# Eight adjacency units of a graph network's first pass go back into their own rows, and VectorE instead of TensorE sums them

## The chip, the cores and the metric

The kernel runs on one core of a Trainium2 chip. The metric is the device time of one execution in microseconds, the median of the runs.

## The reference

Four graph layers over one dense matrix adj of 8192 x 8192 float32 (256 MB) and node states x of 8192 x 64. Each layer normalises x, multiplies adj with the result and adds something made of the product to x, so layer l + 1 needs all of layer l for the columns that it reads:

```python
h = jnp.maximum(_layernorm(x, axis=-1), 0.0)
x = x + _L0_gnn_ref(h, adj, L0_gnn_u)               # adj @ (h * keep / 0.9)
h = jnp.maximum(_layernorm(x, axis=-1), 0.0)
x = x + _L1_gnn_ref(h, adj, L1_gnn_W, L1_gnn_b)     # (adj @ h + h) / deg, then W, relu, norm
h = jnp.maximum(_layernorm(x, axis=-1), 0.0)
x = x + _L2_gnn_ref(h, adj, L2_gnn_W)               # dinv * ((adj + I) @ (dinv * h)) @ W
h = jnp.maximum(_layernorm(x, axis=-1), 0.0)
x = x + _L3_gnn_ref(h, adj, L3_gnn_W)               # concat(h, adj @ h / (deg + 1)) @ W.T
```

The degrees deg are the row sums of adj, needed from layer 1 on.

## The kernel before, in words

adj is cut into 16 x 16 units of 512 x 512 (1 MB each). Unit (b, g) holds what row block b takes from source block g. The kernel makes several passes over the matrix; the change touches only the first (keys that begin with 1), some 760 of the 1857 us. In it the rows b = 0 to 15 are done in turn. For row b:

- the singles, sources g = 15 down to b + 1 (SINGLES): only layer 0 can take them, since the states of layer 1 for block g don't exist yet. `alone` (lines 783 to 791) makes 4 products of them, in one bank's lower half and another's upper half; the two halves of TensorE's columns work side by side.
- the late sources, g = 0 to b - 1 (LATE_SOURCES): here layer 1 is known too, and `both` (lines 793 to 800) makes 8 products of each, layer 0 in the lower half, layer 1 in the upper half of one bank, LOW[b]. A product is two instructions in the trace, so a single has 8 and a unit of both layers 16.
- the diagonal unit, which has two loads' slots of its own, with the layer 1 part of the row before.
- `finish(0, b - 1)` (line 830) after the first single of row b: it turns the sums of the row before for VectorE, which makes the next states of them (lines 1427 to 1432).

The degrees need the sum of every unit once. VectorE adds the units of DVE_SUMS into row_sum (line 1579, and line 1585 for the diagonal), and folds the row's sum at its end (lines 1590 and 1592), after which it begins the next row. After 5 sums of a row it ends layer 0 of the row before, with line 1431 and lines up to 1601. TensorE instead sums the units of PE_SUMS with `count_unit` (lines 840 to 844): 4 small products with a picking matrix into the bank DEG. In rows 4, 8 and 12, after the second single, `count_totals` (lines 846 to 852) adds VectorE's four folded rows to the same bank; it waits for the fold of the row before (total_ready).

The two orders that matter are written out by hand: `loads_in_order` (lines 236 to 253) is SP's order of loads, and TensorE's loop (lines 1195 to 1240) is its order of use. Loads go into a ring of 12 slots; SP loads slot n again when unit n - 12 has been released by TensorE (unit_freed) and, where VectorE sums it, by VectorE (unit_summed, lines 531 to 537).

Before the change two units each of rows 10 and 9 are taken out of their turn in each of rows 1 to 4 (EARLY): in row b, after the singles with index 8 and 9, come units (10, b - 1) and (9, b - 1). TensorE counts them and multiplies them for both layers into banks 4 and 6 (LOW[10], LOW[9]), which nothing else uses till rows 9 and 10 come. So rows 1 to 4 have 18 loads each, rows 9 and 10 have 12.

Of the kernel before, what the change touches and what calls it, by code (L numbers as in the profile page):

```python
# [9 lines left out]
ROWS = 16  # L10
# [20 lines left out]
SINGLES = [list(range(LAST, b, -1)) for b in range(ROWS)]  # L31

EARLY_ROWS = (10, 9)
EARLY = {b: [(r, b - 1) for r in EARLY_ROWS] for b in range(1, 5)}
AFTER_SINGLE = (8, 9)
EARLY_SOURCES = {b: [g for r, g in sum(EARLY.values(), []) if r == b] for b in range(ROWS)}
LATE_SOURCES = [[g for g in range(b) if g not in EARLY_SOURCES[b]] for b in range(ROWS)]
LOW = [b % 2 for b in range(ROWS)]  # L40
LOW[10], LOW[9] = 4, 6

PE_SUMS = [SINGLES[0][1:7]] + [EARLY_SOURCES[b] for b in range(1, ROWS)]
DVE_SUMS = [[g for g in SINGLES[b] + list(range(b)) if g not in PE_SUMS[b]] for b in range(ROWS)]


# [5 lines left out]
def upper(job):  # L52
    return LAST - 1 - job[0], LAST - job[1]


def lower(job):
    return job
# [35 lines left out]
def step_loads(p, kind, n):  # L93

    hi, lo = PAIRS[p]
    if kind == "cover":
        return [(2, 0, n)]
    if kind == "four":
        s1, s2 = FOURS[p][n]
        return [(2, lo, s1), (2, lo, s2), (2, hi, s1), (2, hi, s2)]  # L100
    if kind == "near":
        return [("again", *PAIRS[p - 1][::-1]) if p else (2, 0, CUT), (2, lo, hi)]
    return [(2, hi, n), (2, lo, n)]
# [132 lines left out]
def loads_in_order():  # L236
    out = []
    for b in range(ROWS):
        for i, g in enumerate(SINGLES[b]):
            out += [(1, b, g)]  # L240
            if b in EARLY and i in AFTER_SINGLE:
                out += [(1, *EARLY[b][AFTER_SINGLE.index(i)])]
        out += [(1, b, g) for g in LATE_SOURCES[b][:-1]] + [("diag", 1, b)]
        out += [(1, b, b - 1)] if b else []
    out += [(2, *upper(job)) for step in FIRST_A + FIRST_C for job in step]
    for p, (hi, lo) in enumerate(PAIRS):
        for kind, n in PAIR_STEPS[p]:
            out += step_loads(p, kind, n)
    out += [(2, 0, g) for g in COVER_AT_END[:-1]] + [("again", *PAIRS[-1][::-1]), ("again", 0, CUT),
                                                  (2, 0, COVER_AT_END[-1])]  # L250
    out += [(3, *lower(job)) for step in FIRST_A + FIRST_C for job in step]
    return out + down_loads()
# [35 lines left out]
def gnn_stack(nc, x_in, u_in, stream_in, w1_in, b1_in, w2_in, w3_in, x_out):  # L288
# [6 lines left out]
    with ctx:  # L295
# [111 lines left out]
        def half_of(bank, half):  # L407
            return banks[bank][half * F:(half + 1) * F, :]
# [50 lines left out]
        def source_tile(buf, k):  # L459
            return buf[:, k * COLS:(k + 1) * COLS]  # L460

        def slot(key):
            return ring[PLACE[key] % RING]

        def loaded(key):
            return unit_loaded[PLACE[key] % RING], 16 * (PLACE[key] // RING + 1)
# [4 lines left out]
        def diag_arrived(phase, b):  # L471
            n = DIAGS["diag", phase, b]
            return diag_loaded[n % 2], 16 * (n // 2 + 1)
# [7 lines left out]
        def state(layer, b):  # L481

            return h_ready, 1 + PROLOGUE.index(b // TPR) if layer == 0 else QUARTERS + rank(layer - 1, b) + 1
# [290 lines left out]
        def _(pe):  # L774
            def mm(bank, half, layer, J, moving, start, stop):
                return nc.tensor.matmul(half_of(bank, half), h[layer % 2][:, J], moving, start=start, stop=stop)  # L776

            def await_unit(key, *layers):
                pe.wait_ge(*loaded(key))
                for layer in layers:  # L780
                    pe.wait_ge(*state(layer, key[2]))

            def alone(key, layer, low, high, first, last_low, last_high, fresh_low=True):

                for k in (0, 2):
                    J = key[2] * TPR + k
                    mm(low, 0, layer, J, source_tile(slot(key), k), first and fresh_low and k == 0,
                       last_low and k == 2)
                    done = mm(high, 1, layer, J + 1, source_tile(slot(key), k + 1),
                              first and k == 0, last_high and k == 2)  # L790
                done.then_inc(unit_freed, 1)

            def both(key, layer, bank, first, first_next, last, last_next):

                for k in range(TPR):
                    J = key[2] * TPR + k
                    mm(bank, 0, layer, J, source_tile(slot(key), k), first and k == 0, last and k == TPR - 1)
                    done = mm(bank, 1, layer + 1, J, source_tile(slot(key), k),
                              first_next and k == 0, last_next and k == TPR - 1)
                done.then_inc(unit_freed, 1)  # L800
# [35 lines left out]
            def pick(b):  # L836

                return picker[:, F - 1 - b:F - 1 - b + QUARTER]

            def count_unit(key):  # L840

                for k in range(TPR):
                    nc.tensor.matmul(DEG[k * QUARTER:(k + 1) * QUARTER, :], pick(key[1]), source_tile(slot(key), k),
                                     start=key == (1, 0, PE_SUMS[0][0]), stop=False)

# [350 lines left out]
            for b in range(ROWS):  # L1196
                low, high = LOW[b], 2 + b % 2
                if b >= 2:
                    pe.wait_ge(*gathered(0, b - 2))
                for i, g in enumerate(SINGLES[b]):  # L1200
                    await_unit((1, b, g), 0)
                    if g in PE_SUMS[b]:
                        count_unit((1, b, g))
                    alone((1, b, g), 0, low, high, i == 0, False, b > 0 and g == b + 1, not EARLY_SOURCES[b])
                    if i == min(1, LAST - 1 - b) and b > 0 and b % QUARTERS == 0:
                        count_totals(b - 1)
                    if i == 0 and b > 0:
                        finish(0, b - 1)
                    if b in EARLY and i in AFTER_SINGLE:
                        key = (1, *EARLY[b][AFTER_SINGLE.index(i)])  # L1210
                        await_unit(key, 0, 1)
                        count_unit(key)
                        both(key, 0, LOW[key[1]], b == 1, b == 1, False, False)
                if b >= 2:
                    pe.wait_ge(part_copied, PARTS.index((1, b - 2)) + 1)
                for g in LATE_SOURCES[b][:-1]:
                    await_unit((1, b, g), 0, 1)
                    both((1, b, g), 0, low, b == LAST and g == 0, g == 0, False, False)
                    if b == LAST and g == 0:
                        finish(0, b - 1)  # L1220
                    if b == LAST and g == 10:
                        count_totals(LAST)
                    if b == LAST and g == 11:
                        turn_degrees()
                    if b == LAST and g in (12, 13):
                        turn_own(1, 26 - g)
                pe.wait_ge(*diag_arrived(1, b))
                if b == 0:
                    for k in (0, 2):
                        mm(low, 0, 0, k, source_tile(diag_slot(1, b), k), False, k == 2)  # L1230
                        done = mm(high, 1, 0, k + 1, source_tile(diag_slot(1, b), k + 1), False, k == 2)
                    done.then_inc(diag_used, 1)
                else:
                    pe.wait_ge(diag_plus_one, b)
                    pe.wait_ge(*state(1, b - 1))
                    for k in range(TPR):
                        used = mm(low, 0, 0, b * TPR + k, source_tile(diag_slot(1, b), k), False, False)
                        done = mm(LOW[b - 1], 1, 1, (b - 1) * TPR + k, source_tile(diag_slot(1, b - 1), k),
                                  b == 1 and k == 0, k == TPR - 1)
                    used.then_inc(diag_used, 1)  # L1240
                    done.then_inc(diag_freed, 1)
                    if b == LAST:
                        turn_own(1, 12)
                    await_unit((1, b, b - 1), 0, 1)
                    both((1, b, b - 1), 0, low, False, b == 1, True, False)
# [10 lines left out]
            for k in (0, 1):  # L1256
                J = LAST * TPR + k
# [640 lines left out]
```

## Time and profile before

| | before |
|---|---|
| median of 3 runs | 1855.67 us (1855.26 to 1856.03) |
| the profiled execution | 1858.4 us, its span 1856.6 us |
| TensorE matmul busy | 1806.5 us, 97% |
| VectorE busy | 1461.4 us, 79% |
| DMA, mean | 365 GB/s |
| granted TensorE clock | 0.998 of full speed |

A row of the profile gives a group of instructions by line, engine, operation and what it writes and reads. Busy time is that of at least one instruction running; matmuls overlap, so the starts are a better measure than the sum of durations. In a timeline the number in brackets is the engine's idle time before, with what ended it.

### The profile page before, as it was taken

The page shows a single profiled execution, that of the slowest core. Times are in us where ns is not written, and L with a number is a line of the kernel's source. Part 1 is how long each engine was busy: PE and PEld are TensorE (multiplying, and loading weights), DVE is VectorE, ACT ScalarE, POOL GpSimd, SP SyncE. Part 2 cuts the span into 40 slices and gives each one's busy share as a digit, 9 for nine tenths or more (in the row PEclk, how much of TensorE's full clock was granted, in tenths as well). Part 3 has the DMA queues.
Part 4 walks back from the last instruction along what each step waited for, and adds up shares of the span by engine and source line. Part 5 has one row for each costly group of instructions (what it writes and reads, how often), then busy time and mean ns, then how long its engine had stood idle before and what let it go on. Part 6 is the DMA issues. An engine that isn't in the chain of part 4 may idle for free.

```text
span 1856.6 us, 21067 instructions
## 1 busy us (share of the span) xinstructions
PE 1806.5 (97%) x8392; PEld 624.2 (34%) x8392; DVE 1461.4 (79%) x1529; ACT 102.1 (6%) x270; POOL 9.1 (0%) x23
## 2 busy tenths in 40 slices
PE   5899999999999999999999999999999999999998
PEld 1223333333333333333333333333333333333333
DVE  8989899999997765669888664678878787877754
ACT  0000000000000000100000000111000000000000
POOL 0000000000000000000000000000000000000000
PEclk9999999999999999999999999999999999999999
DMA  9999999999988878298797798499899999999995
GB/s 384 421 421 421 421 421 421 421 421 421 416 333 319 318 282 298 70 408 329 293 393 317 302 365 333 167 366 420 347 422 374 421 383 421 421 393 421 421 421 236
DMA packets 96047, 676.79 MB, mean 365 GB/s; under 512 B 11216, under 2 KB 13264, under 8 KB 14288
## 3 DMA queue, kind: packets, MB, share of 16 engines
q1 hardware_dynamic: 93024, 673.23, 89.1%
q10 hardware_dynamic: 2928, 2.23, 0.4%
q8 instruction: 68, 1.11, 0.2%
q14 instruction: 27, 0.22, 0.0%
HBM read 673.32 MB, written 2.10 MB: 364 GB/s over the span
## 4 chain that ended last, share of the span: by engine, by line
PE 88%; DMA 7%; DVE 4%; issue 0%; SPq 0%; ACT 0%; DVEq 0%
PE acc L776 43%; DMA ring<-stream_in 7%; PE acc L976 5%; PE acc L950 5%; PE DEG L932 4%; PE acc L806 3%; PE HT L776 2%; PE acc L963 2%; PE Z L832 2%; PE acc L1162 2%; PE DEG L1174 2%; PE acc L1079 2%; PE acc L1055 2%; PE acc L1069 2%; PE acc L1110 1%; PE acc L1117 1%
## 5 line engine op out<-in xcount | busy, mean ns | idle before, releaser
L776 PE MATMUL acc<-ring,states 128*64 128x512 f32 x3984 | 901.7, 595 | 33.7 <-DMA ring<-stream_in 29.1
L776 PEld LDWEIGHTS acc<-ring,states 128*64 128x64 f32 x3984 | 286.8, 137 | 583.3 <-issue 553.3
L1579 DVE TENSOR_TENSOR row_sum<-row_sum,ring 128x2048 f32<-128x2048 f32 x194 | 444.6, 2292 | 14.7 <-DMA ring<-stream_in 9.7
L1703 DVE TENSOR_TENSOR ring<-row_totals,ring 128x2048 f32<-128x2048 f32 x27 | 61.8, 2289 | 56.1 <-PE DEG L934 55.9
L932 PE MATMUL DEG<-ring,states 128*64 128x512 f32 x216 | 99.2, 602 | 3.6 <-DMA ring<-stream_in 3.6
L950 PE MATMUL acc<-row_totals,row_sum 128*64 128x512 f32 x216 | 97.3, 593 | 2.7 <-DVE row_sum L1695 2.7
L934 PE MATMUL DEG<-ring,states 128*64 128x512 f32 x216 | 99.3, 603 | 0.0
L978 PE MATMUL acc<-ring,states 128*64 128x512 f32 x216 | 97.7, 595 | 0.0
L976 PE MATMUL acc<-ring,row_sum 128*64 128x512 f32 x216 | 97.7, 595 | 0.0
L952 PE MATMUL acc<-ring,row_sum 128*64 128x512 f32 x216 | 97.3, 593 | 0.0
L776 PE MATMUL acc<-diag,states 128*64 128x512 f32 x336 | 91.1, 594 | 0.6 <-DMA diag<-stream_in 0.6
L1675 DVE TENSOR_TENSOR row_totals<-ring 128x2048 f32<-128x2048 f32 x27 | 61.8, 2290 | 4.4 <-DMA ring<-stream_in 2.8
L1679 DVE TENSOR_TENSOR ring<-ring 128x2048 f32<-128x2048 f32 x27 | 61.9, 2292 | 1.1
L1712 DVE TENSOR_TENSOR ring<-ring 128x2048 f32<-128x2048 f32 x27 | 61.9, 2292 | 0.9
L832 PEld LDWEIGHTS Z<-below,y 128*128 128x128 f32 x384 | 47.0, 191 | 40.2 <-issue 28.0
L1657 DVE TENSOR_TENSOR y<-acc,y 64x512 f32<-64x512 f32 x65 | 44.4, 682 | 17.6 <-PE acc L776 15.5
L832 PE MATMUL Z<-below,y 128*128 128x64 f32 x384 | 52.4, 279 | 3.8 <-DVE y L1658 3.8
L950 PEld LDWEIGHTS acc<-row_totals,row_sum 128*64 128x64 f32 x216 | 29.2, 137 | 65.0 <-issue 57.3
L806 PE MATMUL acc<-ring,states 128*128 128x512 f32 x112 | 50.9, 601 | 0.0
L963 PE MATMUL acc<-ring,row_sum 128*64 128x512 f32 x108 | 50.7, 592 | 0.0
L965 PE MATMUL acc<-ring,row_sum 128*64 128x512 f32 x108 | 50.7, 592 | 0.0
L932 PEld LDWEIGHTS DEG<-ring,states 128*64 128x64 f32 x216 | 29.2, 139 | 63.7 <-issue 63.4
(207 smaller groups left out, 2087.0 us busy)
## 6 DMA issues: line engine op xcount, KB each, us to landing
ring<-stream_in SPq DMA_DIRECT2D x610, 1024.0 KB, 12.5
diag<-stream_in SPq DMA_DIRECT2D x28, 1024.0 KB, 13.2
x<-x_in SPq DMA_DIRECT2D x4, 512.0 KB, 7.0
y<-u_in SPq DMA_DIRECT2D x4, 512.0 KB, 8.9
x_out<-x ACTq DMA_DIRECT2D x16, 128.0 KB, 6.7
below<-w_in ACTq DMA_DIRECT2D x6, 16.0 KB, 5.7
bias<-b_in ACTq DMA_DIRECT2D x1, 32.0 KB, 10.0
```

The source lines that it names most:

```text
L776: return nc.tensor.matmul(half_of(bank, half), h[layer % 2][:, J], moving, start=start, stop=stop)
L806: done = nc.tensor.matmul(acc[bank][:, :], states[:, J * 2 * F:(J + 1) * 2 * F], source_tile(slot(key), k), start=first and k == 0, stop=l ...
L832: mm_z = nc.tensor.matmul(Z[:, t * F:(t + 1) * F], gathered_sums, below[:, layer - 1, :], start=True, stop=True)
L932: nc.tensor.matmul(down("P2"), h[0][:, a12[2] * TPR + k], source_tile(slot(a12), k), start=i == 0 and k == 0, stop=False)
L934: one = nc.tensor.matmul(down("P1"), h[0][:, a11[2] * TPR + k], source_tile(slot(a11), k), start=i == 0 and k == 0, stop=last and k == TPR ...
L950: nc.tensor.matmul(down("P5"), down_state(1)[:, k], source_tile(row_totals, k), start=i == 0 and k == 0, stop=last and k == TPR - 1)
L952: seven = nc.tensor.matmul(down("P7"), down_state(3)[:, k], source_tile(slot(a21), k), start=i == 0 and k == 0, stop=last and k == TPR - 1)
L963: nc.tensor.matmul(down("P4"), down_state(4)[:, k], source_tile(slot(a22), k), start=i == 0 and k == 0, stop=False)
L976: nc.tensor.matmul(down("P6"), down_state(2)[:, k], source_tile(slot(a11), k), start=i == 0 and k == 0, stop=last and k == TPR - 1)
L978: three = nc.tensor.matmul(down("P3"), h[1][:, a12[2] * TPR + k], source_tile(slot(a12), k), start=i == 0 and k == 0, stop=last and k == T ...
L1579: nc.vector.tensor_tensor(row_sum[:, :], before, slot(key)[:, :], ALU.add).then_inc(unit_summed, 1 if count > 1 else 2)
L1679: nc.vector.tensor_tensor(slot(a21)[:, :], slot(a11)[:, :], slot(a21)[:, :], ALU.subtract).then_inc(down_formed, 1)
```

## The change

The eight units stay in their own rows. The tables EARLY, AFTER_SINGLE and EARLY_SOURCES go, LATE_SOURCES holds all sources, all rows use banks 0 and 1, and PE_SUMS is empty apart from six units of row 0, so that DVE_SUMS holds the eight units. The loads and TensorE's loop lose the units in rows 1 to 4. All rows from 1 have 16 loads.

```diff
-EARLY_ROWS = (10, 9)
-EARLY = {b: [(r, b - 1) for r in EARLY_ROWS] for b in range(1, 5)}
-AFTER_SINGLE = (8, 9)
-EARLY_SOURCES = {b: [g for r, g in sum(EARLY.values(), []) if r == b] for b in range(ROWS)}
-LATE_SOURCES = [[g for g in range(b) if g not in EARLY_SOURCES[b]] for b in range(ROWS)]
+LATE_SOURCES = [list(range(b)) for b in range(ROWS)]
 LOW = [b % 2 for b in range(ROWS)]
-LOW[10], LOW[9] = 4, 6
-
-PE_SUMS = [SINGLES[0][1:7]] + [EARLY_SOURCES[b] for b in range(1, ROWS)]
+
+PE_SUMS = [SINGLES[0][1:7]] + [[] for b in range(1, ROWS)]
 DVE_SUMS = [[g for g in SINGLES[b] + list(range(b)) if g not in PE_SUMS[b]] for b in range(ROWS)]
...
         for i, g in enumerate(SINGLES[b]):
             out += [(1, b, g)]
-            if b in EARLY and i in AFTER_SINGLE:
-                out += [(1, *EARLY[b][AFTER_SINGLE.index(i)])]
...
-                    alone((1, b, g), 0, low, high, i == 0, False, b > 0 and g == b + 1, not EARLY_SOURCES[b])
+                    alone((1, b, g), 0, low, high, i == 0, False, b > 0 and g == b + 1)
...
-                    if b in EARLY and i in AFTER_SINGLE:
-                        key = (1, *EARLY[b][AFTER_SINGLE.index(i)])
-                        await_unit(key, 0, 1)
-                        count_unit(key)
-                        both(key, 0, LOW[key[1]], b == 1, b == 1, False, False)
```

`alone` loses its parameter fresh_low, with which rows 9 and 10 went on in a bank that was begun earlier.

## Rows read from the trace of the kernel before

**Rows 1.** The page: engines' busy time and share; GB/s in 40 slices.

```profile
PE 1806.5 (97%) x8392; PEld 624.2 (34%) x8392; DVE 1461.4 (79%) x1529; ACT 102.1 (6%) x270; POOL 9.1 (0%) x23
...
GB/s 384 421 421 421 421 421 421 421 421 421 416 333 319 318 282 298 70 408 329 293 393 317 302 365 333 167 366 420 347 422 374 421 383 421 421 393 421 421 421 236
```

**Rows 2.** Stretches cut by hand: end of row 0, rows 1, 3 and 7.

```profile
core 0: us, PE busy (x) PEld busy (x) DVE busy (x) ACT busy (x) POOL busy (x), PEclk, DMA share, GB/s
...
50.00:62.00 12.00, 9.80 (x44) 2.65 (x40) 10.28 (x6) 1.16 (x2) 0.00 (x0) 1.00 1.02 423
...
62.00:108.00 46.00, 41.63 (x195) 12.06 (x192) 43.23 (x31) 1.95 (x4) 0.00 (x0) 1.00 1.01 420
155.00:202.00 47.00, 45.37 (x217) 14.35 (x216) 42.03 (x29) 1.95 (x4) 0.00 (x0) 1.00 1.01 421
...
328.00:370.00 42.00, 42.00 (x199) 14.16 (x197) 40.75 (x30) 1.95 (x4) 0.00 (x0) 1.00 1.01 421
```

**Rows 3.** TensorE's waits (total us, times, longest): whole span, then 174 to 760 us.

```profile
PE acc L776 <- DMA ring<-stream_in: 29.1, 19, 19.6
...
PE acc L776 <- issue: 0.3, 1, 0.3
```

**Rows 4.** TensorE's timeline in rows 0 and 3 (start, duration, work, idle before).

```profile
57.23 1.94 PE L776 MATMUL acc<-diag,states 128*64 128x512 f32 x8 [0.55 <-DMA diag<-stream_in]
...
171.89 1.07 PE L843 MATMUL DEG<-ring,picker 128*32 128x512 f32 x8 [0.54 <-DMA ring<-stream_in]
172.89 5.37 PE L776 MATMUL acc<-ring,states 128*64 128x512 f32 x24
```

**Rows 5.** The chain that ended last, pieces in row 6 and row 11.

```profile
287.91 13.88 PE acc L776 x64
301.79 0.33 issue
...
480.41 48.22 PE acc L776 x224
```

**Rows 6.** VectorE's timeline: first sums of rows 1, 6, 7, 8; sums and fold between.

```profile
63.97 2.29 DVE L1579 TENSOR_TENSOR row_sum<-ring 128x2048 f32<-128x2048 f32 x1
...
237.12 2.29 DVE L1579 TENSOR_TENSOR row_sum<-row_sum,ring 128x2048 f32<-128x2048 f32 x1 [0.20 <-DMA ring<-stream_in]
...
284.31 2.29 DVE L1579 TENSOR_TENSOR row_sum<-ring 128x2048 f32<-128x2048 f32 x1
...
300.60 18.57 DVE L1579 TENSOR_TENSOR row_sum<-row_sum,ring 128x2048 f32<-128x2048 f32 x8
...
325.90 2.29 DVE L1579 TENSOR_TENSOR row_sum<-ring 128x2048 f32<-128x2048 f32 x1
...
366.71 0.69 DVE L1592 TENSOR_TENSOR row_totals<-row_sum 128x512 f32<-128x512 f32 x1
367.49 2.29 DVE L1579 TENSOR_TENSOR row_sum<-ring 128x2048 f32<-128x2048 f32 x1
```

**Rows 7.** TensorE's timeline, line 830 (ends the row before): starts in rows 7 to 12.

```profile
328.02 0.66 PE L830 MATMUL Z<-ident,y 128*128 128x128 f32 x4
369.96 0.66 PE L830 MATMUL Z<-ident,y 128*128 128x128 f32 x4
414.76 0.66 PE L830 MATMUL Z<-ident,y 128*128 128x128 f32 x4
446.40 0.66 PE L830 MATMUL Z<-ident,y 128*128 128x128 f32 x4
479.75 0.66 PE L830 MATMUL Z<-ident,y 128*128 128x128 f32 x4
528.56 0.66 PE L830 MATMUL Z<-ident,y 128*128 128x128 f32 x4
```

**Rows 8.** TensorE's timeline at the count of totals in row 8.

```profile
372.41 1.07 PE L851 MATMUL DEG<-row_totals,picker 128*32 128x512 f32 x8
```

**Rows 9.** Groups by line and form, 0 to 650 us: the counts of units.

```profile
L843 PE MATMUL DEG<-ring,picker 128*32 128x512 f32 x112 | 15.3, 617 | 1.7 <-DMA ring<-stream_in 1.7
```

More of the change, by code:

```diff
@@ L781, in await_unit, with alone @@
                     pe.wait_ge(*state(layer, key[2]))
-            def alone(key, layer, low, high, first, last_low, last_high, fresh_low=True):
+            def alone(key, layer, low, high, first, last_low, last_high):
                 for k in (0, 2):
                     J = key[2] * TPR + k
-                    mm(low, 0, layer, J, source_tile(slot(key), k), first and fresh_low and k == 0,
+                    mm(low, 0, layer, J, source_tile(slot(key), k), first and k == 0,
                        last_low and k == 2)
```

## The prediction

> **What bounds the kernel now.** I read the page first, its shares and its slices. The reader is to see that TensorE is busy nearly throughout and that the transfers run at 421 GB/s for the first quarter of the span and never again for so long [rows 1]. Then the stretches cut at the row boundaries: TensorE has idle time in rows 1 and 3 of the first pass and none in row 7, where VectorE is busy 40.8 us of 42 and the transfers still run at 421 GB/s; the granted clock is 1.00 everywhere [rows 2]. The waits say the same: TensorE lost 29.1 us to landings at line 776 in 19 waits, of which 19.57 us is the start, and after 174 us of the first pass nothing but 0.3 us of issue [rows 3]. So there are three suppliers of almost equal pace. A unit of the matrix lands every 2.49 us: TensorE's starved units start at 57.23 and 171.89 us, which are loads 15 and 61 of the stream counted from 0, so (171.89 - 57.23) / 46 = 2.493 us [rows 4]. A single (lines 783 to 791) takes TensorE 1.72 us (8 of them 13.88 us less one drain), a unit for both layers 3.44 us (224 instructions in 48.22 us, 16 to a unit) [rows 5]. A whole row takes VectorE 41.59 us where it waits for nothing: its first sums of rows 6 to 8 start 41.59 us apart [rows 6]. Sixteen landings take 16 x 2.49 = 39.8 us, so VectorE is slower than the landings in a row with no extra units. TensorE needs 29.8 + 1.72 b us for row b with all its sources (15 - b singles, b + 1 of both layers with the diagonal, 0.6 us of line 830); the traced starts of line 830 agree (row 7: 41.94; row 11: 48.81) [rows 7]. It is therefore below the landings up to row 5 and above from row 6.
>
> **Part 1, the eight units leave rows 1 to 4.** Each row has 16 landings instead of 18. TensorE is given 2 x 3.44 us of products and 2 x 1.00 us of counts less in each (a count of a unit, line 843, is 8 instructions; the next work starts 1.00 us after it) [rows 4]. All that was work in a stretch where it waits for landings at the end of the singles, so the removed work is worth nothing there; the landings are. After the change the last single of row b is load 16 b + 14 - b, and TensorE starts it when it lands or when its own work is done. Row 4: load 74 lands at about 204.9 us. From there 1.72 + 0.33 us (the single, and the gap in front of the units of both layers [rows 5]), 5 x 3.44 us of both layers, then nine singles and line 830 of row 5 (16.1 us) put the last single of row 5 at 240.2; it (load 89) lands at 242.1, so TensorE is starved. From that, 1.72 + 0.33 + 6 x 3.44 + 8 x 1.72 + 0.6 gives 279.2 for the last single of row 6; it is load 104, which lands at 237.12 + 17 x 2.49 = 279.4 (237.12 is the start of VectorE's sum of load 87, which it waited for) [rows 6]. So starvation ends just there, at 279.4. Before, TensorE starts the same single at 301.79 - 1.94 = 299.9 [rows 5]. TensorE is 20.5 us earlier at this place. That is about the eight landings (19.9 us).
>
> **Part 2, the eight units arrive in rows 9 and 10.** Both rows lie where TensorE has no idle time [rows 3], so each unit costs its full 3.44 us: 8 x 3.444 = 27.6 us. The rows took 31.64 and 33.35 us with 12 units (line 830 to line 830) [rows 7]; they become 45.4 and 47.1. Without anything else the sum would be 27.6 - 20.5 = 7.1 us slower. The landings don't hold these rows up: TensorE is some 17 us behind them in row 9, 22 in row 10 and 30 in row 11, which a ring of 12 slots (29.9 us of landings) still covers.
>
> **Part 3, VectorE sums the eight units.** 8 x 2.33 = 18.6 us more work [rows 6]. In rows 9 and 10 it is beside TensorE's longer rows (41.59 against 45.4 and 47.1 us), hence no cost. But in rows 1 to 4 VectorE loses what it had before: 18 landings (44.8 us) to do 41.59 us of work, with waits for the ring behind most sums [rows 6]. With 16 landings it never waits again. Its first sum of row 1 starts at 63.97 as before (row 0 is unchanged); the fifth needs load 21 (72.2 us) at 73.3, the closest place; from then it falls 1.8 us a row further behind the landings. So its row b starts at 63.97 + 41.59 (b - 1), row 4 at 188.7 and row 8 at 355.1.
>
> **Part 4, who waits for that.** Line 846, count_totals, makes TensorE wait in rows 4, 8 and 12, after the second single, for the fold of the row before on VectorE, and everything of TensorE's queue stands behind it. Row 4: TensorE comes there at about 187.1, the fold is ready at 188.6; the 1.6 us vanish, as it is starved later in that row. Row 8: in the trace of before the way from the last single of row 6 (299.9) to the count of row 8 (372.41) is 72.5 us [rows 5, 8], so TensorE comes to it at 279.4 + 72.5 = 351.9. The fold is ready at 355.0, 0.1 before the next row's first sum, and TensorE goes on at 355.1. Before, VectorE's fold was ready at 367.4 and TensorE came at 372.4, so this wait hid itself with 5 us to spare [rows 6, 8]. It is a new stall of 3.2 us, and no starvation comes later to absorb it. Row 12: VectorE at 521.5, TensorE at about 541, no wait. TensorE at the count of row 8 is thus 372.4 - 355.1 = 17.3 us earlier than before, and 27.6 - 17.3 = 10.2 us later after row 10.
>
> **Part 5, banks and what follows.** Rows 9 and 10 accumulate in banks 1 and 0 of all other rows, and take their waits for copies by ScalarE; neighbouring rows show no idle time for them [rows 3], so I cost it at 0 (bounds 0 and 0.3 us, the one issue gap). The pass ends in TensorE's work with the ring full, before as after, so the shift goes through to the end: nothing later starts from anything but the first pass's results and TensorE's releases. ScalarE and SP get no more to do; SP's loads change order only.
>
> The page on DMA of the Trainium skill (DMA: Bandwidth & Descriptors, Specifications) gives a limit of about 358 GB/s of HBM per core. The first pass moves 421 GB/s for 500 us, so the trace disagrees and decides [rows 1]. By the page a unit would take 2.93 us, the eight landings would be worth 23.4 us and the sum would be +4.1 us with VectorE ahead of the landings.
>
> **The sum.** The profiled execution took 1858.4 us with a span of 1856.6, 2.7 us over the median. +10.2 us gives a span of 1866.8 and a median of 1855.67 + 10.2 = 1865.9 us, 0.55% slower.
>
> **Rivals.** (a) VectorE doesn't gate: its fold of row 7 is ready before 351.9, or comes to be waited for only where there is slack. Then +7.1 us, 1862.8. Against it: a period of 41.59 that the trace repeats to 0.01 us [rows 6]. (b) VectorE is later: in row 1 it has only 1.0 us of margin to the landings, and some landings come 0.4 to 0.6 us late; each microsecond lost there appears as one at row 8. With 0.45 us lost in each of seven rows it is +13.3 us, 1869.0. (c) Faster, the other side: landings aren't what paces rows 4 to 6, TensorE stays fed after row 3 as now, and only its saved counts remain. That is 64 of the 112 count instructions of line 843, in eight units of 1.00 us [rows 4, 9]. Then -8.0 us, 1847.7. It decides where a landing takes less than row 4's work over its 16 units, 37.7 / 16 = 2.36 us; the rows show 2.49. (d) No change to measure: the two effects offset, as the eight landings and the lost wait in row 3 are worth nearly what the late units cost; it wants some 6 us more of gain in rows 1 to 6 than I find, and VectorE not to gate. +1 us, 1856.7.
>
> **How the numbers follow.** The forecast has 66%, with its own range of +9 to +12 us. (a) has 12%, (b) 10%, (c) 6%, (d) 6%. A difference of under 0.2% (3.7 us) can't be told from none by a measurement of this kernel. So faster 0.06, same 0.06, slower 0.88. The range leaves out (c) and (d) and reaches from below (a), 1861.5, to just over (b), 1869.5.
>
> **What would show each step.** Part 1: TensorE is starved in rows 1 to 6, the last time near 280 us, at gaps of 0.5 us that leave its granted clock at 1.00, as the like gaps of row 0 do [rows 2, 4]. Part 2: line 830 to line 830 of rows 9 and 10 at 45.4 and 47.1 us. Part 3: VectorE's first sums 41.59 us apart from 63.97 on, with no wait for the ring in between. Part 4: line 851 in row 8 starts near 355 and waited about 3 us for VectorE, with row 8's line 830 at about 349. If the first sum of row 8 starts before 352, (a) holds; if the last starved single is well before 240 us, (c) or (d) does; a wait of TensorE in rows 9 to 15 would break part 2 and make it slower still.

## The result, and the profile after

The changed kernel takes 1865.71 us (median of 4 runs, 1863.67 to 1867.1) against 1855.85 for the one before, a ratio of 1.0049 with a 95% interval of 1.0036 to 1.0061. That is 9.9 us slower, where 10.2 was forecast. The profiled execution took 1867.1 us with a span of 1865.2, against 1858.4 and 1856.6.

The page of the changed kernel, the lines that answer to [rows 1]:

```profile
span 1865.2 us, 20963 instructions
...
PE 1803.0 (97%) x8328; PEld 626.2 (34%) x8328; DVE 1479.7 (79%) x1537; ACT 102.0 (5%) x270; POOL 9.1 (0%) x23
...
GB/s 384 422 421 421 421 421 420 421 420 392 349 341 314 302 310 306 65 392 318 337 360 313 312 355 352 150 403 413 350 420 374 421 384 421 421 392 421 421 421 233
```

TensorE has 64 instructions less (the counts) and is busy 3.5 us less, VectorE 18.3 us more (eight sums), and the span is longer all the same. The transfers leave 421 GB/s a slice earlier, since TensorE falls behind them in rows 9 and 10: between 420 and 470 us SP waits 36.4 us for TensorE's releases of slots and 5.8 us for VectorE's.

TensorE's waits in the changed kernel (total us, times, longest), to lay beside [rows 3]; 19.3 us of the first line are again the start:

```profile
PE acc L769 <- DMA ring<-stream_in: 37.7, 36, 19.3
...
PE DEG L844 <- DVE row_totals L1580: 3.4, 2, 2.2
PE acc L769 <- issue: 3.4, 5, 1.0
```

36 waits for landings instead of 19, and one of a new kind: line 844 (line 851 before) waits for VectorE's folds. TensorE's timeline of the changed kernel from the end of row 6's singles, with line 823 (830 before) where it ends a row and line 844 at row 8's count:

```profile
267.40 13.95 PE L769 MATMUL acc<-ring,states 128*64 128x512 f32 x64
282.34 17.39 PE L769 MATMUL acc<-ring,states 128*64 128x512 f32 x80 [0.99 <-issue]
...
350.18 0.66 PE L823 MATMUL Z<-ident,y 128*128 128x128 f32 x4
350.77 1.94 PE L769 MATMUL acc<-ring,states 128*64 128x512 f32 x8
354.88 1.58 PE L844 MATMUL DEG<-row_totals,picker 128*32 128x512 f32 x8 [2.17 <-DVE row_totals L1580]
356.39 33.96 PE L769 MATMUL acc<-ring,states 128*64 128x512 f32 x152
...
398.87 0.66 PE L823 MATMUL Z<-ident,y 128*128 128x128 f32 x4
444.24 0.66 PE L823 MATMUL Z<-ident,y 128*128 128x128 f32 x4
491.33 0.66 PE L823 MATMUL Z<-ident,y 128*128 128x128 f32 x4
...
758.03 0.66 PE L823 MATMUL Z<-ident,y 128*128 128x128 f32 x4
```

The last line is the end of the first pass; in the kernel before it stands at 746.46. VectorE's first sums of rows 1, 7 and 8 (beside [rows 6]):

```profile
63.78 2.29 DVE L1567 TENSOR_TENSOR row_sum<-ring 128x2048 f32<-128x2048 f32 x1
...
313.32 2.29 DVE L1567 TENSOR_TENSOR row_sum<-ring 128x2048 f32<-128x2048 f32 x1
354.91 2.29 DVE L1567 TENSOR_TENSOR row_sum<-ring 128x2048 f32<-128x2048 f32 x1
```

(354.91 - 63.78) / 7 = 41.59 us a row: from row 1 to row 8 VectorE waits for no landing. Its only waits there are eight for ScalarE of at most 0.3 us each, which it had before too. The count at 354.88 starts when its fold is ready.

The difference of the two traces adds up place by place. At row 8's count TensorE is 372.41 - 354.88 = 17.5 us earlier. From there to the end of row 8 it takes 398.87 - 354.88 = 43.99 us, where it took 414.76 - 372.41 = 42.35: 1.6 us more. Rows 9 and 10 take 45.37 and 47.09 us instead of 31.64 and 33.35: 27.5 us more. Sum: 11.6 us later at the end of the pass (758.03 against 746.46). By the end of the span it is 8.6 us; the 3.0 us between have a section of their own below.

The 1.6 us in row 8 are TensorE's clock. Stretches of the changed kernel around the count, columns as in [rows 2]:

```profile
353.00:356.00 3.00, 1.12 (x8) 0.16 (x8) 2.88 (x3) 0.00 (x0) 0.00 (x0) 0.88 1.00 418
356.00:360.00 4.00, 4.00 (x16) 1.19 (x14) 3.93 (x3) 0.00 (x0) 0.00 (x0) 0.66 1.02 420
360.00:364.00 4.00, 4.00 (x20) 1.26 (x18) 3.97 (x2) 0.00 (x0) 0.00 (x0) 1.00 1.00 418
```

Just behind the wait of 2.17 us the granted clock is 0.66 as a mean of a stretch, that is at its lower level (1.2 of 2.4 GHz) for a part of it, and full again after.

### The profile page after: what moved, and what is told of

The parts are those of the page before. It is cut to its first block, busy times and chain, and to the rows that moved or that the text cites. A ratio compares the mean times of both kernels' runs of the same rounds, so it can differ in the third digit from the quotient of the medians.

```text
span 1865.2 us, 20963 instructions
## 1 busy us (share of the span) xinstructions
PE 1803.0 (97%) x8328; PEld 626.2 (34%) x8328; DVE 1479.7 (79%) x1537; ACT 102.0 (5%) x270; POOL 9.1 (0%) x23
## 4 chain that ended last, share of the span: by engine, by line
PE 76%; DVE 19%; DMA 3%; issue 1%; SPq 0%; ACT 0%; DVEq 0%
PE acc L769 35%; DVE row_sum L1567 12%; PE acc L969 5%; PE acc L943 5%; PE DEG L925 4%; PE acc L799 3%; PE Z L825 2%; PE acc L956 2%; DMA ring<-stream_in 2%; PE acc L1155 2%; PE DEG L1167 2%; PE acc L1072 2%; PE acc L1048 2%; PE acc L1062 2%; PE acc L1103 1%; PE acc L1110 1%
## 5 line engine op out<-in xcount | busy, mean ns | idle before, releaser
L769 PE MATMUL acc<-ring,states 128*64 128x512 f32 x4152 | 937.0, 596 | 45.4 <-DMA ring<-stream_in 37.7
L769 PEld LDWEIGHTS acc<-ring,states 128*64 128x64 f32 x4152 | 299.4, 137 | 625.8 <-issue 571.7
L1567 DVE TENSOR_TENSOR row_sum<-row_sum,ring 128x2048 f32<-128x2048 f32 x202 | 462.9, 2292 | 6.4
L971 PE MATMUL acc<-ring,states 128*64 128x512 f32 x216 | 97.7, 595 | 0.0
```

What stands on the lines that cost most here:

```text
L971: three = nc.tensor.matmul(down("P3"), h[1][:, a12[2] * TPR + k], source_tile(slot(a12), k), start=i == 0 and k == 0, stop=last and k == T ...
L1567: nc.vector.tensor_tensor(row_sum[:, :], before, slot(key)[:, :], ALU.add).then_inc(unit_summed, 1 if count > 1 else 2)
```

## The experiments

The start of line 830 (line 823 in the changed kernel) that ends the first pass (near 750 us) is a sharper measure than the time, as it doesn't contain what happens in the later passes. Each experiment has both. Compared with it: 746.46 in the kernel before, 758.03 in the changed one.

**The changed kernel once more** (no edit).

> The changed kernel unaltered, for a second trace and a narrower interval. My theory: TensorE is starved to about 282 us, waits some 2 to 3 us at the count of totals in row 8 for VectorE's fold, the granted clock falls just behind that wait in some executions and not in others (up to 1.6 us), and the first pass ends 10 to 11.6 us later than before. What came back at about 1200 us in the first trace (11.6 us became 8.2) is chance in how transfers start again after a pause: it will be another amount here. The rival, that it comes back by mechanism: the first pass ends 11.6 later and 3.4 us come back at the same place again. Median 1865 to 1866.

Measured 1865.57 us, ratio 1.0049 (1.0035 to 1.0063). The same stall in TensorE's timeline, and a stretch behind it with the lowered clock:

```profile
354.52 1.07 PE L844 MATMUL DEG<-row_totals,picker 128*32 128x512 f32 x8 [2.42 <-DVE row_totals L1580]
```

```profile
355.00:360.00 5.00, 5.00 (x22) 1.46 (x16) 4.93 (x3) 0.00 (x0) 0.00 (x0) 0.66 1.01 421
```

The first pass ends at 757.74, 11.3 us after that of before. From there to the end of the span both traces of this kernel take 1107.1 to 1107.2 us, the one of before 1110.1. So the forecast of another amount was wrong: on the changed kernel's side it was the same.

The expectation also said that the clock falls behind this wait in some executions and not in others. The traces can't show that, as both have the fall, but the mean granted clock of every execution is on record to three decimals. Of the nine executions of the changed kernel (four above, five here) four have 0.998 and took 1866.74 to 1867.1 us, both traced ones among them; five have 0.999 and took 1863.67 to 1865.57 us. In all 13 traces of this case the clock is lowered at the end of the span, which takes at least 1.4 us' worth of full clock (the kernel with ten early units has a mean of 0.70 from 1850 us to its end at 1854.9). A fall like the one at the stall takes 1.7 us more, 3.1 together. A mean that rounds to 0.999 leaves at most 2.8. So it is very likely that five of the nine executions had the wait without the fall of the clock; they are 2.0 us shorter in the mean, and the medians lie among them or just above. This is inferred, since there is no trace of such an execution.

**Totals counted later** in the changed kernel: after the fifth single instead of the second in rows 4 and 8 (row 12 has only three singles, and counts after the third).

```diff
-                    if i == min(1, LAST - 1 - b) and b > 0 and b % QUARTERS == 0:
+                    if i == min(4, LAST - 1 - b) and b > 0 and b % QUARTERS == 0:
```

> The changed kernel, but in rows 4 and 8 TensorE counts the totals after the fifth single instead of the second (row 12: after the third). If the wait for VectorE's fold in row 8 is a term of its own: TensorE comes there 5.2 us later, after the fold (354.9), so the 2.2 us wait and the 1.6 us of lowered clock behind it are gone: 2.2 to 3.8 us faster than the changed kernel, 7 to 7.8 us slower than before, no wait at that line, clock 1.00 through row 8. If the wait is only a symptom and the landings or the banks of rows 9 and 10 hold the pass: no difference from the changed kernel.

Measured 1862.37 us (1861.92 to 1862.72), ratio 1.0030 (1.0019 to 1.0042); 3.2 us faster than the changed kernel in the same series. The first pass ends at 753.22. Row 8's count, in the timeline, and the stretch behind the old place of the wait:

```profile
356.85 1.06 PE L844 MATMUL DEG<-row_totals,picker 128*32 128x512 f32 x8
```

```profile
355.00:360.00 5.00, 5.00 (x28) 1.36 (x26) 4.93 (x3) 0.00 (x0) 0.00 (x0) 1.00 1.00 415
```

No wait, full clock. The stall is a term of its own, of 3.2 us in the time and 4.5 us between the trace of the rerun and this one (757.74 - 753.22: the wait of 2.4, the clock of 1.7, and 0.3 us of a landing's jitter at the start). The rest, 753.22 - 746.46 = 6.8 us, is what the eight late units cost in rows 9 and 10 less what the eight landings save, without VectorE; it was forecast as 7.1. The 3.2 and the 4.5 us agree with the two kinds of execution: these six executions (all at a mean clock of 0.999) have a median 3.0 us under the rerun's three at 0.999, which is the wait, and 4.6 us under its two at 0.998, which is the wait with the lowered clock.

**VectorE relieved**: TensorE counts one single in each of rows 1 to 4 of the changed kernel.

```diff
-PE_SUMS = [SINGLES[0][1:7]] + [[] for b in range(1, ROWS)]
+PE_SUMS = [SINGLES[0][1:7]] + [SINGLES[b][8:9] if b < 5 else [] for b in range(1, ROWS)]
```

> The changed kernel, but TensorE counts one single (the ninth) in each of rows 1 to 4, so that VectorE has 4 sums less (9.3 us) there. If VectorE's 41.59 us a row against 39.8 us of landings causes the wait in row 8: its row 8 begins at about 347 instead of 354.9, the wait is gone, and the time is that of the kernel with late totals (7 to 7.8 us over before); the 4 us of counts that TensorE gets cost nothing, as it is starved in those rows. If TensorE's own work in rows 1 to 4 counts: 4 us slower than that.

Measured 1862.74 us, ratio 1.0032 (1.0019 to 1.0045). VectorE's row 8 begins at 347.00 and TensorE counts without a wait; the first pass ends at 753.04, within 0.2 us of the kernel with late totals. VectorE's first sum of row 8, then TensorE's count:

```profile
347.00 2.29 DVE L1567 TENSOR_TENSOR row_sum<-ring 128x2048 f32<-128x2048 f32 x1
```

```profile
351.53 1.07 PE L844 MATMUL DEG<-row_totals,picker 128*32 128x512 f32 x8
```

Two different edits, one to TensorE's order and one to VectorE's load, take away the same stall. It also shows that 4 us of work put on a starved TensorE cost nothing.

**More work for VectorE** in row 5 of the changed kernel, five small multiplications without use:

```diff
+                    if i == 5 and b == 5:
+                        for _ in range(5):
+                            chain(nc.vector.tensor_tensor(squares[:, :], centred[:, :], centred[:, :], ALU.mult))
                     if i == 5 and b > 0:
                         end_layer_0(b - 1)
```

> The changed kernel, with 2.3 us of work without use on VectorE in row 5 (five small multiplications). If row 8's count waits for VectorE, each microsecond is passed on: VectorE's row 8 begins at 357.2, the wait is 4.5 instead of 2.2 us, and the time is 2.3 us over the changed kernel. If VectorE has slack: no difference.

Measured 1869.63 us, 4.1 us over the rerun in the other series, ratio to before 1.0075 (1.0060 to 1.0090). VectorE's row 8 begins at 356.54, 2.0 us after the rerun's 354.56, the wait is 4.09 us and the first pass ends 1.7 us later than the rerun's. So in the trace the delay is passed on nearly one to one. The time rose by more than the trace shows, so the dose was doubled.

**Twice that** (range(10)).

> The changed kernel with ten small multiplications without use on VectorE in row 5, twice those of the kernel with more work for VectorE (whose row 8 began 2.0 us later). VectorE's row 8 begins 4 us later than in the changed kernel, at 358.5 to 359; TensorE waits about 6.2 us in row 8; the first pass ends 4 to 4.6 us later than the changed kernel's, the granted clock falls behind the wait as at waits of 2.2 us and more. If the cost of a wait is only its length, 4 us over the changed kernel; if a longer wait also keeps the clock low for longer, up to 6 us.

Measured 1871.92 us, ratio 1.0079 (1.0066 to 1.0091); 6.4 us over the rerun. VectorE's row 8 begins at 359.04, 4.5 us later; the wait is longer by 4.8 us and the pass ends at 762.43, 4.7 us later. The count in TensorE's timeline, then two stretches:

```profile
359.01 1.94 PE L844 MATMUL DEG<-row_totals,picker 128*32 128x512 f32 x8 [7.25 <-DVE row_totals L1580]
```

```profile
355.00:360.00 5.00, 0.99 (x8) 0.20 (x8) 4.84 (x4) 0.00 (x0) 0.00 (x0) 0.62 1.02 424
360.00:365.00 5.00, 5.00 (x24) 1.36 (x18) 4.93 (x3) 0.00 (x0) 0.00 (x0) 0.70 0.99 401
```

The clock is lowered in two stretches now, but row 8 from count to end takes 44.26 us against 44.05. The reason is where the lowered stretch lies. Cut finer, the clock has a mean of 0.59 from 356 to 357 us and is at its lower level from there to 363, so it fell some 2.8 us before the count started at 359.01, and about 4 us of it had work. In the rerun it fell after the wait had ended.

Both medians exceed the traces' shift by 1.7 to 2.4 us. A large part of that is the kind of execution. Three of the four executions with more work and all five with twice that have a mean clock of 0.997 or 0.996, at least 4.6 us' worth of lowered clock, where no trace has more than 3.2 at the end of the span; so the clock fell in them at the stall or elsewhere. The rerun's median is one without the fall. Against its two executions at 0.998 (1866.93 and 1867.0) the medians are 2.7 and 4.9 us longer, and the shifts in the traces are 1.7 and 4.7. The remaining 1.0 and 0.2 us can't be told from the difference between the series, in which the kernel before itself had medians of 1856.33 to 1857.65.

**TensorE counts the eight units** where they now are.

```diff
-PE_SUMS = [SINGLES[0][1:7]] + [[] for b in range(1, ROWS)]
+PE_SUMS = [SINGLES[0][1:7]] + [list(range(4)) if b in (9, 10) else [] for b in range(1, ROWS)]
...
                     await_unit((1, b, g), 0, 1)
+                    if g in PE_SUMS[b]:
+                        count_unit((1, b, g))
                     both((1, b, g), 0, low, b == LAST and g == 0, g == 0, False, False)
```

> The changed kernel, but TensorE counts the eight units in rows 9 and 10, as it did before in rows 1 to 4, and VectorE doesn't sum them. If TensorE is the bound in rows 9 and 10 and VectorE's eight sums are hidden there: each count costs its full 1.0 us, 8 us slower than the changed kernel, 18 us slower than before. If VectorE's 18.6 us of sums cost anything in those rows, the difference is smaller than 8 us or has the other sign.

Measured 1877.04 us, ratio 1.0111 (1.0097 to 1.0125); 11.5 us over the changed kernel, not 8. Line 823 at the ends of rows 8, 9 and 10, and the count of row 8 ahead of them:

```profile
354.25 1.06 PE L844 MATMUL DEG<-row_totals,picker 128*32 128x512 f32 x8 [1.94 <-DVE row_totals L1582]
...
396.60 0.66 PE L823 MATMUL Z<-ident,y 128*128 128x128 f32 x4
446.56 0.66 PE L823 MATMUL Z<-ident,y 128*128 128x128 f32 x4
498.24 0.66 PE L823 MATMUL Z<-ident,y 128*128 128x128 f32 x4
```

Rows 9 and 10 take 49.96 and 51.68 us instead of 45.37 and 47.09, so four counts cost 4.6 us, 1.15 each and not the 1.0 that the start of the next work gave in row 3. VectorE's eight sums are hidden in these rows: without them TensorE gains nothing. Row 8 has a wait of 1.94 us and full clock behind it, and takes 42.35 us, exactly as before. The first pass ends 7.2 us after the rerun's (9.2 of counts, less 1.7 of clock and 0.3 us of jitter), and another 2.9 us are lost later, at the place that the section on the 3.0 us is about. That is 10.1 us in the traces; the traced execution (1876.68) is the second shortest of four that reach to 1878.77, so 1.4 us of the median's 11.5 lie in no trace.

**Six units stay early** (range(1, 4) in EARLY of the kernel before).

> The kernel before, but without early units in row 4: six stay early, two go back to rows 9 and 10. By the ledger of landings (each unit that moves saves 2.49 us of landing where TensorE is starved and costs 3.44 us where it isn't), TensorE starts the last single of row 6 at 294.9 instead of 299.9 and the pass ends 1.9 us later than before; VectorE's fold is in time in row 8 by some 3 us. By TensorE's own work (two counts of 1.0 us saved, no starvation after row 3): 2 us faster than before.

The first pass ends at 748.12, 1.7 us later than before. Time 1856.41 against 1856.33, ratio 1.0007 (0.9997 to 1.0016), which can't be told from none; it does exclude a gain of 2 us.

**Four units stay early**: EARLY_ROWS = (10,), AFTER_SINGLE = (8,), LOW[10] = 4.

> The kernel before, but only row 10's units are taken early, one in each of rows 1 to 4; row 9 has all 16 in turn. By the ledger of landings: last single of row 6 at 289.9, the pass ends 4 x 0.95 = 3.8 us later than before; VectorE's row 8 begins near 357, TensorE comes at 362, no wait. By TensorE's own work (four counts saved): 4 us faster.

The first pass ends at 750.86, 4.4 us later. Time 1859.01, ratio 1.0014 (1.0004 to 1.0023). The sign is that of the landings: by TensorE's saved counts it would have been 4 us faster.

**The early units aren't counted** (line 1212 of the kernel before, count_unit(key), is left out).

> The kernel before, but TensorE doesn't count the eight early units; nobody does, so the degrees of rows 9 and 10 lack them. That takes 8.0 us of work from TensorE in rows 1 to 4 and nothing from the landings. If landings pace it up to row 6 even in the kernel before (it reaches the units of both layers of row 6 at 302.1, with load 113 landing at about 301.8), the gain is 0 to 1 us. If only the starvation seen up to 172 us counts, the four counts behind it are a gain of 4 us; if all TensorE's work counts, 8 us.

Measured 1856.18 against 1856.33 us, ratio 0.9999 (0.9989 to 1.0008), which excludes a gain of 4 or 8 us; the first pass ends at 746.19 instead of 746.46. Eight microseconds of TensorE's work were worth nothing, though TensorE showed no idle time from row 4 on in the trace of before [rows 3]. The reason is visible in its waits: total us, times and longest of this kernel's landings.

```profile
PE acc L776 <- DMA ring<-stream_in: 33.2, 28, 19.3
```

28 waits where before had 19: much of the work taken away shows again as starvation (each wait shows some 0.2 us less than it lasts: a starved single's record lasts 1.94 us, where the next one of a series starts 1.72 after it). And the kernel before was still paced by landings at 302 us. TensorE's first units of both layers in row 6, in the kernel before and then without the counts:

```profile
302.12 17.39 PE L776 MATMUL acc<-ring,states 128*64 128x512 f32 x80 [0.33 <-issue]
```

```profile
301.59 17.39 PE L776 MATMUL acc<-ring,states 128*64 128x512 f32 x80 [0.26 <-issue]
```

The view gives these gaps to "issue", but in the traces load 113 landed at 302.03 and 301.50 us, 0.09 us ahead of each start. In every trace that has such a gap at the end of row 6's singles, TensorE starts 0.09 to 0.10 us after the landing of the load that it needs there. So everything taken from TensorE ahead of this place is filled up again by the wait for load 113, and the reading of the 0.33 us as idle time without a cause [rows 3, 5] was wrong.

**Ten units early** (range(1, 6) in EARLY).

> The kernel before with two more early units, (10, 4) and (9, 4) in row 5: ten in all. The ledger of landings says that moving a unit late costs 0.95 us only while TensorE is starved afterwards; at eight early units its starvation behind row 6 is down to 0.3 us. So two more bring no gain: row 5 gets 8.9 us of work (two units at 3.44 and two counts at 1.0), rows 9 and 10 lose 6.9, and the pass ends 1.7 to 2.0 us later than before. If the gain of 0.95 us a unit went on beyond eight, it would be 1.9 us faster than before.

The first pass ends at 748.08, 1.6 us later. Time 1857.23 against 1857.65, ratio 1.0000 (0.9991 to 1.0008), an interval from 1.7 us faster to 1.5 us slower. So the time excludes a gain of 1.9 us, but it doesn't show the loss of 1.6 us either, which rests on one trace. In that trace TensorE has no wait at all between 236 and 420 us, the first kernel here that is no longer held up by landings at the end of row 6's singles. The ends of the pass side by side (0 units: the changed kernel with late totals, as it has no stall):

| early units | 10 | 8 (before) | 6 | 4 | 0 |
|---|---|---|---|---|---|
| last line 830 (823), us | 748.08 | 746.46 | 748.12 | 750.86 | 753.22 |
| over before | 1.6 | 0 | 1.7 | 4.4 | 6.8 |
| expected | 1.7 to 2.0 | 0 | 1.9 | 3.8 | 7.1 |

The last line of TensorE's timeline of the pass with ten units, and with four:

```profile
748.08 0.66 PE L830 MATMUL Z<-ident,y 128*128 128x128 f32 x4
```

```profile
750.86 0.66 PE L830 MATMUL Z<-ident,y 128*128 128x128 f32 x4
```

By the end of the first pass eight is the best of these numbers; by the time, six, eight and ten can't be told apart, and no version here is faster than the kernel before by more than the noise.

**Totals counted later in the kernel before**, the same edit.

> The kernel before with the totals counted after the fifth single in rows 4 and 8. There VectorE's fold of row 7 was ready 5 us ahead of TensorE, so no wait goes: no difference (within 0.1%). If a late count were of use by itself, 3 us faster as on the changed kernel.

1856.15 against 1857.65 us, ratio 0.9993 (0.9984 to 1.0002), pass end 746.37 against 746.46. A late count is of no use where there is no wait.

## The 3.0 us that came back after the first pass

The time from the first pass's end to the end of the span is 1110.1 us in the profiled execution of before, but 1107.1 to 1107.2 in both traces of the changed kernel. Most of it lies near 1200 us, where the transfers start again after a pause and TensorE waits for the first of them. TensorE's waits for landings between 1100 and 1300 us and the stretch of 1190 to 1230 us, in the kernel before:

```profile
PE DEG L932 <- DMA ring<-stream_in: 2.4, 1, 2.4
```

```profile
1190.00:1230.00 40.00, 37.60 (x170) 13.30 (x168) 29.12 (x39) 6.01 (x15) 0.00 (x0) 0.96 0.76 311
```

and the same in the changed kernel:

```profile
PE DEG L925 <- DMA ring<-stream_in: 0.7, 1, 0.7
```

```profile
1190.00:1230.00 40.00, 38.11 (x189) 15.22 (x184) 28.63 (x50) 7.97 (x20) 0.00 (x0) 1.00 0.47 192
```

The wait is 2.4 us with a clock mean of 0.96 in the one, 0.7 us at full clock in the other. Over all 13 traces it lies between 0.7 and 2.4 us. It was 2.4 in the kernel before, 2.0 in the same with the late count and in the one where TensorE counts the eight units, and 1.1 or less in the ten others. It goes neither with the change nor with the end of the first pass, so I count it as no part of the change; but why it is long in some kernels stays open, and one trace each can't tell a kernel's property from an execution's. The traced execution of the kernel before is 2.7 us over its median, though (1858.4 against 1855.67), and it is the only one of the six versions of that kernel with a lowered clock at this place; from the pass's end on it takes 1110.1 us, the other five 1106.8 to 1108.1. So most of the 3.0 us is probably of this one execution, and not in the median.

## Why the prediction was right, point by point

- **Part 1, landings pace TensorE up to row 6.** Right, to 0.1 us: the last single of row 6 was forecast at 279.4; it is the eighth of the eight from 267.40, 267.40 + 7 x 1.72 = 279.4. TensorE doesn't wait there, since load 104 landed at 279.06; by its own work it was forecast at 279.2, so the two limits lay too close to tell. The claim that removed work is worth nothing there is shown by the kernel without counts. What the step had wrong is small: it took the 0.33 us ahead of the units of both layers for a fixed gap, and it is a wait for a landing. In the changed kernel that gap is 0.59 us in rows 4 and 5. In row 6 it is 0.99 us in the first trace, where load 105 landed 3.19 us after load 104, and 0.25 to 0.30 in the six other traces of that kernel and its variants.
- **Part 2, 3.44 us for each unit in rows 9 and 10.** Right: forecast 45.4 and 47.1, measured 45.37 and 47.09.
- **Part 3, VectorE runs without waits at 41.59 us a row.** Right: row 8 at 354.91, forecast 355.1. Its sums in rows 9 and 10 are hidden, as the kernel with TensorE's counts shows.
- **Part 4, the new stall at row 8.** Right in place and releaser, a little large in size: 2.2 to 2.4 us in two traces, forecast 3.2. TensorE came 0.2 to 0.8 us later than computed, most of the 0.8 the late landing of part 1, and VectorE 0.2 to 0.6 us earlier. Only VectorE's error reaches the sum: where the fold sets the start, it doesn't matter when TensorE came. Taking the wait away in two ways gives 2.8 and 3.2 us in the time. The stall in row 4 (forecast 1.6, measured 1.25) was absorbed.
- **The clock** was the term left out. The text expected 1.00 at the gaps of 0.5 us, which is so, and put no clock term on its own stall of 3.2 us. In both traces the clock was lowered behind it, which cost 1.6 to 1.7 us; by the mean clocks this happened in about half of the executions. The forecast's own range of 9 to 12 us still holds the 11.6 of the pass's end.
- **The sum.** At the end of the pass the forecast of 10.2 is measured as 11.3 to 11.6; in the median as 9.9, and in the rerun as 8.9 (1865.57 - 1856.65). Without the lowered clock the traces' 11.3 to 11.6 would be 9.6 to 9.9, so the forecast's terms describe the executions without the fall, and the medians lie with them. That the first median comes within 0.2 us of the forecast is luck in part, as the rerun's 8.9 shows, and so is that the executions split as they do: had the clock fallen in most of them, the forecast would have been short by a clock term.
- **Rivals.** (a), no gate by VectorE, is what the two edits produce on purpose, 1862.4 to 1862.7 against its 1862.8. (b) is wrong: no wait for landings between VectorE's sums. (c), that TensorE's saved counts decide, fell with the kernels without counts and with six and four units. (d) fell with the result.

## What to carry to other kernels

Where a transfer stream, one engine and another have nearly the same pace, price a moved piece of work by what bounds the place it leaves and the place it goes to: here 2.49 us of landing saved against 3.44 us of TensorE's work paid, 0.95 us a unit by these numbers and 0.8 to 1.1 by the ends of the pass with six, four and no early units, and nothing for counts done by a starved engine. An engine that shows almost no idle time can still be paced by landings: taking 8 us of work from it changed nothing, as one gap of 0.33 us at 302 us was the last wait of a long series. Look at what landed just ahead of such a gap, also where the view names no releaser. And when a stretch gets shorter for one engine, look for the next wait that crosses to another engine whose pace didn't change; moving that wait three units down the queue gave 3 us back.

## What the runs showed of the hardware

In the traces TensorE's clock fell to its lower level at single waits of 2.17, 2.42, 4.09 and 7.25 us at the same place in otherwise busy work, but not at one of 1.94 us there. With the two shorter waits it fell once the work had started again, with the 4.09 us one 0.4 us and with the 7.25 us one 2.8 us before the wait's end. By the mean clocks of the other executions the fall came in only about half of those with the short wait, so a wait of this length doesn't bring it each time. Waits of 0.2 to 0.7 us for one landing after another in rows 1 to 5 of the changed kernel, and one of 1.25 us in row 4, left the granted clock at 1.00 (mean from 24 to 353 us). Where the clock fell, it cost 1.4 to 1.9 us at all four (row 8 from the count to its end in 43.75 to 44.26 us against 42.35), so a wait of 2.2 to 2.4 us cost some 1.7 times its length. Near 1200 us, in another mix of work, a wait of 2.0 us came both with a lowered clock (where TensorE counts the eight units, mean 0.96) and without.

A stream of 1 MB loads kept one every 2.49 us (421 GB/s) for 400 us, but single loads came late: load 105 of the first trace 3.19 us after the one before. TensorE started on a load 0.09 to 0.10 us after its landing where it waited for one at the end of row 6's singles.
